# The reciprocal roots of a perceiver's batch loop: from ScalarE's Sqrt to Newton steps on VectorE

## The reference, cut to what matters

```
xn  = layernorm(context, ln_x_g, ln_x_b)          # rows of 512
ln  = layernorm(layernorm(x), ln_l_g, ln_l_b)
q   = ln @ Wq ;  k, v = (concat(xn, ln) @ Wkv)    # 822 keys
out = softmax(mask(q k^T / 8)) v                  # 16 heads
x   = x + tanh(g) * layernorm(out @ Wout, ln_o_g, ln_o_b)
layernorm(t) = (t - mean(t)) * rsqrt(var(t) + 1e-5)
```

## Time and profile before

| | us |
|---|---|
| median of 3 runs | 2095.2 (2090.87 to 2096.77) |
| the profiled execution | 2099.28, its span 2097.6 |
| PE busy | 1910.5 (91%) |
| DVE busy | 1021.2 (49%) |
| ACT busy | 845.9 (40%) |
| POOL busy | 640.9 (31%) |

### The profile page before, as it was taken

The page is one execution under the profiler, slowest core; times in us unless marked ns, Lnnn a source line. Parts: engine busy times, 40 slices in busy tenths (PEclk is TensorE's granted clock), DMA queues, the critical chain, the costliest instruction groups (busy, mean ns, idle before and its releaser), DMA issues. The chain is left out here.

```text
span 2097.6 us, 35149 instructions
## 1 busy us (share of the span) xinstructions
PE 1910.5 (91%) x12136; PEld 1551.3 (74%) x12136; DVE 1021.2 (49%) x2213; ACT 845.9 (40%) x1776; POOL 640.9 (31%) x519
## 2 busy tenths in 40 slices
PE   5689999999999999999859999999997885999994
PEld 3367878777777778787648888888884665999983
DVE  5324646464645555554464323333336556554564
ACT  3134434443434434434434323333322534565550
POOL 1203020202020020200034445555422203688872
PEclk9799999999999999999969999999998986999997
DMA  8642121211121212100053313333349125454646
GB/s 223 191 162 67 53 58 53 62 53 30 42 69 37 77 37 59 27 17 18 5 185 114 109 59 109 110 105 110 120 157 307 41 69 183 146 201 152 209 144 204
DMA packets 125590, 218.84 MB, mean 104 GB/s; under 512 B 40335, under 2 KB 41135, under 8 KB 124931
## 3 DMA queue, kind: packets, MB, share of 16 engines
q1 hardware_dynamic: 120643, 201.21, 29.8%
q0 software_dynamic: 4800, 15.73, 2.2%
HBM read 188.87 MB, written 28.04 MB: 103 GB/s over the span
## 5 line engine op out<-in xcount | busy, mean ns | idle before, releaser
L485 POOL TENSOR_TENSOR a_cols<-a_cols,a_moments_b 128x722 f32<-128x722 f32 x32 | 57.4, 1792 | 600.3 <-DMA a_moments_b<-a_moments_dram 600.3
L641 PE MATMUL a_kv_ps<-a_kvin_hi,a_wk_hi 128*128 128x512 f32 (+1 forms) x512 | 196.9, 385 | 12.3 <-DVE a_kvin_lo L889 12.3
L1094 PE MATMUL f_banks<-f_wab_hi,f_x_hi 128*128 x448 | 183.6, 410 | 2.8 <-DVE f_x_lo L1781 2.3
L643 PE MATMUL a_kv_ps<-a_kvin_hi,a_wk_lo 128*128 128x512 f32 (+1 forms) x512 | 180.6, 353 | 0.0
L642 PE MATMUL a_kv_ps<-a_kvin_lo,a_wk_hi 128*128 128x512 f32 (+1 forms) x512 | 180.4, 352 | 0.0
L1096 PE MATMUL f_banks<-f_wab_hi,f_x_lo 128*128 x448 | 176.4, 394 | 0.0
L1095 PE MATMUL f_banks<-f_wab_lo,f_x_hi 128*128 x448 | 175.9, 393 | 0.0
L563 ACT ACTIVATE a_probs<-a_probs,a_neg_max 100x822 f32<-100x822 f32 x128 | 125.9, 984 | 118.6 <-DVE a_neg_max L913 118.4
L1803 DVE TENSOR_TENSOR f_h_sb<-f_h_sb,f_banks 128x256 f32<-128x256 f32 x112 | 47.2, 421 | 239.9 <-ACT f_h_sb L1526 237.5
L1526 ACT ACTIVATE f_h_sb<-f_banks 128x256 f32<-128x256 f32 x112 | 43.1, 385 | 292.0 <-PE f_banks L1096 288.0
L641 PE MATMUL a_kv_ps<-a_wv_hi,a_kvin_hi 128*128 128x512 f32 (+1 forms) x384 | 157.2, 409 | 3.3 <-DVE a_k_lo L906 3.3
(11 more groups left out here) (409 smaller groups left out, 4825.2 us busy)
## 6 DMA issues: line engine op xcount, KB each, us to landing
f_raw<-f_pieces SPq DMA_DIRECT2D x94, 256.0 KB, 2.6
m_raw<-m_pieces SPq DMA_DIRECT2D x92, 256.0 KB, 2.8
f_wab_raw<-f_pieces SPq DMA_DIRECT2D x42, 512.0 KB, 6.2
m_wab_raw<-m_pieces SPq DMA_DIRECT2D x42, 512.0 KB, 6.1
a_cols<-ctx_cols SPq DMA_DIRECT2D x8, 1444.0 KB, 7.7
a_rows<-ctx SPq DMA_DIRECT2D x8, 1280.0 KB
a_moments_b<-a_moments_dram SPq DMA_DIRECT2D x8, 722.0 KB
ahead_piece<-g_ctx SPq DMA_DIRECT2D x2, 2880.0 KB, 20.4
```

The lines of the kernel that those rows point to most:

```text
L641: nc.tensor.matmul(out, hi_l, hi_r, start=first, stop=False)
L643: return nc.tensor.matmul(out, lo_l, hi_r, start=False, stop=last)
L1094: nc.tensor.matmul(out, left_hi, right_hi, start=start, stop=False)
```

## The change

In the loop, VectorE computes the reciprocal root by itself. `spread_rooted` adds epsilon, forms minus half of the variance, takes the first guess from the bits (a shift by one, then a constant minus the result, on integers), and makes 3 Newton steps y = y (1.5 - 0.5 v y y) of three instructions each: 13 instructions, 12 of them linked. ScalarE's `deviations` calls in the loop are gone. The roots before the loop and after it stay with ScalarE, with the number to wait for as an argument.

The place moves as well: before, VectorE's reciprocal stood at the head of the step after (pair 1, 3, 6); now the chain stands at the end of pair 0, 2, 5, behind the second division.

```
+            def spread_rooted(first, end):
+                m = slice(first, end)
+                var, y, h = mean_var[:, m, 1], root[:, m], less_half[:, m]
                 dev[0] += 1
-                dve.wait_ge(std_done, dev[0])
+                dve.wait_ge(var_done, dev[0])
+                own.link(nc.vector.tensor_scalar(var, var, EPS, None, ALU.add))
+                nc.vector.tensor_scalar(h, var, -0.5, None, ALU.mult)
+                own.link(nc.vector.tensor_scalar(y.bitcast(I32), var.bitcast(I32), 1, None, ALU.logical_shift_right))
+                own.link(nc.vector.tensor_scalar(y.bitcast(I32), y.bitcast(I32), -1.0, float(0x5F3759DF), ALU.mult, ALU.add))
+                for step in range(STEPS):
+                    own.link(nc.vector.tensor_tensor(var, y, y, ALU.mult))
+                    own.link(nc.vector.tensor_tensor(var, var, h, ALU.mult))
+                    own.link(nc.vector.scalar_tensor_tensor(var if step == STEPS - 1 else y, var, 1.5, y, ALU.add, ALU.mult))
...
-                    if hp == 0:
-                        if i + 1 < B:
-                            deviations(0, CT + 1)
-                        else:
-                            deviations(NEXT_IN, NEXT_IN + 1)
-                    if hp == 2 and i:
-                        deviations(OUT, OUT + 1)
-                    if hp == 5 and i == B - 1:
-                        deviations(NEXT_IN, NEXT_IN + 1)
...
-                    if hp == 1:
-                        if i + 1 < B:
-                            spread(0, CT + 1)
-                            dve.sem_inc(moments_done, 1)
-                        else:
-                            spread(NEXT_IN, NEXT_IN + 1)
-                        if i >= 2:
-                            normalise_next(i - 2)
+                    if hp == 1 and i >= 2:
+                        normalise_next(i - 2)
...
                     if hp == 3 and i:
-                        spread(OUT, OUT + 1)
                         finish(i - 1)
...
+                    if hp == 0:
+                        if i + 1 < B:
+                            spread_rooted(0, CT + 1)
+                            dve.sem_inc(moments_done, 1)
+                        else:
+                            spread_rooted(NEXT_IN, NEXT_IN + 1)
+                    if hp == 2 and i:
+                        spread_rooted(OUT, OUT + 1)
+                    if hp == 5 and i == B - 1:
+                        spread_rooted(NEXT_IN, NEXT_IN + 1)
```

More of the change, by code:

```diff
@@ L7 @@
 U8 = mybir.dt.uint8
+I32 = mybir.dt.int32
 ALU = mybir.AluOpType
@@ L154, in perceiver_attention @@
         std = sb("std", [P, CT + 2])
+        root = sb("root", [P, CT + 2])
+        less_half = sb("less_half", [P, CT + 2])
         l_stats = sb("l_stats", [P, B, 6])
@@ L241, in perceiver_attention @@
         halves = (slice(0, HD), slice(HD, P))
+        STEPS = 3
+        VARS = 2 * B + 3
         OWN = [2, 1, 2, 1, 1, 1, 0, 0]
@@ L505, in _, with deviations @@
             act.wait_ge(const_done, 5)
[L506 to L511, removed]
+            def deviations(n, first, end):
+                act.wait_ge(var_done, n)
                 nc.scalar.activation(std[:, first:end], mean_var[:, first:end, 1], ACT.Sqrt, bias=eps[:, :]).then_inc(std_done, 1)
@@ L585, in _ @@
                                      bias=bias_l[:, k:k + 1]).then_inc(lat_t_done, 1)
-            deviations(0, CT)
+            deviations(1, 0, CT)
             for u in range(PAIRS):
@@ L632, in _ @@
             move_t(PAIRS * B - 1, 1)
-            deviations(OUT, OUT + 1)
-            deviations(NEXT_IN, NEXT_IN + 1)
+            deviations(VARS - 1, OUT, OUT + 1)
+            deviations(VARS, NEXT_IN, NEXT_IN + 1)
             move_next(B - 1)
@@ L863, in _ @@
             dev = [0]
-            def wait_std():
+            def spread_rooted(first, end):
+                m = slice(first, end)
+                var, y, h = mean_var[:, m, 1], root[:, m], less_half[:, m]
                 dev[0] += 1
-                dve.wait_ge(std_done, dev[0])
+                dve.wait_ge(var_done, dev[0])
[7 more added lines that the diff above has]
+                    own.link(nc.vector.scalar_tensor_tensor(var if step == STEPS - 1 else y, var, 1.5, y, ALU.add, ALU.mult))
             def moments(p, tiles):
@@ L879, in moments, with spread @@
                 return ins
-            def spread(first, end):
-                wait_std()
+            def spread(n, first, end):
+                dev[0] += 1
+                dve.wait_ge(std_done, n)
                 own.link(nc.vector.reciprocal(mean_var[:, first:end, 1], std[:, first:end]))
@@ L1007, in _ @@
             moments(0, range(CT)).then_inc(var_done, 1)
-            spread(0, CT)
+            spread(1, 0, CT)
             dve.sem_inc(moments_done, 1)
@@ L1082, in _ @@
             project(B - 1).then_inc(var_done, 1)
-            spread(OUT, OUT + 1)
+            spread(2, OUT, OUT + 1)
             finish(B - 1)
@@ L1086, in _ @@
             moments_next(B)
-            spread(NEXT_IN, NEXT_IN + 1)
+            spread(3, NEXT_IN, NEXT_IN + 1)
             normalise_next(B - 1)
+            assert dev[0] == VARS
             keep_logits(B - 1)
```

## The result

The changed kernel takes 2081.3 us (median of 4 runs, 2081.14 to 2082.74) and the kernel before 2096.0 (4 runs, 2090.87 to 2100.61). The two medians differ by 14.7 us. The ratio on record is 0.9941, with a 95% interval of 0.992 to 0.9962: 12.4 us less, 8 to 17 by the interval. The forecast was 2085 on a median of 2095.2, that is 10.0 less.

A forecast was written before the change was run, and what follows sets the result against it. TensorE, busy 91% of the span, was taken as the bound, so only its waits counted: 6.4 + 1.0 + 2.6 = 10.0 us off the median of 2095.2 gives 2085; range for 8 in 10: 2079 to 2092.

The forecast's parts named there:

- (a): Pair 3, batches 1 to 7: without the Exp table load, seven score waits for the low keys go, 6.4 us.
- (b): Pair 1: batch 0's wait of the values' projection for the low keys goes, 1.0 us; nothing in batches 1 to 7.
- (c): Batch 7, pairs 5 and 6: value-tile wait of 1.32 goes, last score wait falls from 3.73 to 2.45; together 2.6 us.
- (d): The other table loads, behind pairs 0 and 2: worth nothing, since TensorE's work covers them.
- The chain: 13 small VectorE instructions behind pairs 0 and 2: 2.5 us, at most 3.9, hidden under cover, 0 on the path.
- this surplus: Pair 2: waits of 2.3 us where a division meets GpSimd's work on the context columns, to stay as before.
- rival 1: TensorE's clock follows idle times, in the last pair and pair 5: 2080, or 2090 if all five pairs fall; chance 0.14.
- Rival 2: Pair 3: GpSimd's delayed bias step meets VectorE's first division, 0.9 us lost in each of 7, 2091; chance 0.11.
- Rival 3: Pairs 3 and 1: VectorE's chain outlasts its cover of 4.5 and 5.6 us; 2109 at 0.6 an instruction; chance 0.05.
- Rival 4: TensorE never waited for the loads; another input, the copies out of PSUM, keeps the wait: 2095; chance 0.04.
- The sign that I had named against myself: Stages after 1060 us, whose instructions are the same: a length change over a few us would show the forecast wrong.

The follow-up runs named there:

- the moments first: The changed kernel, with SyncE storing and spreading the next batch's moments ahead of its wait for the previous batch's attention: 2080.3 us, ratio 0.9935 to the kernel before.
- the last run: The changed kernel with moments spread before SyncE's attention wait and routing bias added to logits before context columns are prepared: 2065.8 us, ratio 0.9873 to the kernel before.
- 12-step run: The changed kernel with 12 Newton steps instead of 3, 40 small instructions a chain instead of 13: 2111.2 us, ratio 1.0083 to the kernel before.

## Why the prediction was right, step by step

(a) Seven waits of the scores in pair 3, 6.4 us by the earlier trace rows: the pairs lost 0.97 or 0.98 each, 6.8. I take the 0.07 beyond the idle time of 0.90 for what the count of idle time leaves out at its edge; no run shows it apart. Batch 0 as the check of what a pair without a load costs (11.38) was exact.

(b) Pair 1 of batch 0, 1.0: measured 1.2. It keeps its 16.83 where only pair 3's loads go, and is back at 16.81 with all loads back. Pair 1 of the other batches: nothing, as said.

(c) Batch 7, pair 6: 2.6 against 2.9. The wait of 1.32 went, and the last wait fell from 3.73 to this:

```profile
1017.93 0.48 PE L707 MATMUL a_s_ps<-a_k_hi,a_q_hi 64*100 64x512 f32 x2 [2.33 <-DVE a_k_lo L912]
```

2.45 had been forecast. The load there costs 1.40, that is 0.12 more than its own 1.28; what the 0.12 are is open. The 1380 ns of drain that the Trainium skill gives beside a load ("ScalarE: Activation LUTs", "What ACT_TABLE_LOAD costs") would have made this 2.66; the trace disagrees here, where the load has nothing to wait for but the activation before it.

(d) The other loads: nothing. The run with the loads back shows it for pair 0's; for the Sqrt behind pair 2 it is read from ScalarE's idle time.

The chain: 2.38 us against 2.5, in pair 3 with 2.8 us of slack left behind it. The spacing of 0.20 on 8 elements held for 1 and 7 elements and, within 0.02, for the integer steps.

What I did not forecast. Pair 2 grew by 1.0 in the profiles. It moves by the start of GpSimd's work against the division: over the eight profiles with the old order of SyncE's queue pair 2 of batches 1 to 6 scatters between 14.17 and 15.5, and with the moments first it stands still. The forecast called this surplus unchanged. I take it for chance of the execution, of up to 1.3 us a pair: the changed kernel and the one with 48 copies more have the same loop, and their seven pairs take 103.9 and 102.0. Pair 0 of batch 0 was 1.2 shorter; its stretch from 113.5 to 124.5 has a granted clock of 0.53 before and of 0.69 after. It is 47.0 to 47.4 in the eight experiments as well, with the loads (47.22) and without. So the loads are not its cause, and the long one was the profile of before.

The last pair. After the shorter wait TensorE ran at half speed (1.2 GHz of 2.4) for 3.4 us, where before it did so from 1028.3 for 6.8, and the pair up to the end of its stage is 1.3 shorter. The stretch of half speed in the changed kernel:

```profile
1019.00:1022.40 3.40, 3.40 (x37) 2.90 (x34) 0.69 (x2) 0.00 (x0) 0.00 (x0) 0.52 0.00 0
```

That looks like rival 1 on this pair, but the shorter wait isn't the cause. In the run with only the output norm's root replaced the wait is the old one, and yet half speed lasts as briefly as here:

```profile
1017.95 0.47 PE L716 MATMUL a_s_ps<-a_k_hi,a_q_hi 64*100 64x512 f32 x2 [3.73 <-DVE a_k_lo L923]
```

```profile
1019.00:1022.40 3.40, 3.40 (x37) 2.96 (x34) 0.70 (x2) 0.00 (x0) 0.00 (x0) 0.54 0.00 0
```

The last pair takes 27.80 us there and 27.79 with all loads back, also behind 3.73 us of idle, against 27.78 in the changed kernel. In the last run it takes 26.23 behind the same 2.33 as in the changed kernel, and the clock doesn't fall at all:

```profile
1004.00:1007.40 3.40, 3.40 (x40) 2.27 (x37) 0.66 (x2) 0.50 (x1) 0.00 (x0) 1.00 0.00 0
```

So the length of half speed here is not set by the length of the wait, and the 1.3 us came by the luck of the two profiled executions. The clock of pair 5, the other part of the rival, did not move: two of five such pairs fell in both profiles (batches 4 and 5 before, 2 and 6 after). Over the profiles of the kernels that keep these waits it was 1 to 4 of the five, and none where the waits are gone.

The rivals. Rival 1: neither part is shown as an effect of the change. Rival 2: the mechanism exists and missed by 0.34 us in the nearest batch (by 0.6 in batch 4, where 0.3 had been forecast); 1.75 us more of chain bring it, for 0.5 to 0.6 us a pair where 0.9 had been put. The Trainium skill's rule for it ("SBUF — State Buffer", the reading notes on the port diagram) is that of VectorE and GpSimd the one that starts first has the shared pair of ports for its whole instruction and the other is blocked. The trace agrees, for both orders: a division of 0.65 turns to 1.73 beside a bias step of 1.30 that starts 0.01 ahead, and the bias step to 1.74 where the division is ahead by 0.07. Only the price is a little less than the rule would give: the blocked division ends 0.44 us after the bias step, not 0.65. Rival 3: the mechanism is true too, its price was too high. The 12-step run has 2111, where 2109 had been worked out for a chain of 7.2; for its chains of 7.6 behind pair 2 and 8.05 behind pair 0 the same working gives 2118. The cover was 2.4 + 2.8 = 5.2 us behind pair 2 of batch 4 and 2.6 + 3.6 = 6.2 behind pair 0, against 4.5 and 5.6. The prediction had read pair 3 in a profile in which a division of 1.82 us had made pair 2 late (0.4), had taken 0.75 for a normalisation that takes 0.55, and 0.3 off each for no stated reason. Rival 4 falls with the run that has the loads back.

The sign that I had named against myself, stages behind 1060 us changing by more than a few us, came near with 4.3; ten profiles of the same code scatter there by 11 us, so it was too narrow a sign for one pair of executions.

The result lies 3.7 below the forecast, 2.4 by the ratio. Of these 0.9 are in the three terms. The rest is within the interval of the ratio, 8 us wide, and nothing that the change did is known for it: the forecast's mechanism and its terms are shown, and that the whole came out so near is in part luck.

## What to carry to other kernels

A table load costs what the most critical reader behind the next activation loses, not its 1.28 us: of 32 removed, 22 had cost nothing and ten gave 10.9 us, and the number to add up is the idle time in front of the reader, or the load where that is shorter. A chain of small dependent instructions is cheap where its engine already waits for another; work out the slack to the first instruction that another engine waits for, and look which third engine's work the delay pushes onto what. Once a wait is understood, look whether the order in the same engine's program holds others: here one call moved ahead of another was worth as much again as the whole change. And a gain that one pair of profiles shows outside the places of the change is held against the other runs before it gets a cause: here the last pair had a good reason and the wrong one.

## What the runs showed of the hardware

- Small linked VectorE instructions (1 to 7 elements a partition, float or int32) take 0.14 to 0.17 us and start 0.18 to 0.21 apart, up to 39 links in a row.
- A Sqrt on one element a partition with its load costs ScalarE 1.28 + 0.20, and 1.28 again for the next Exp; the load takes 1283 ns at every one of the 32 places.
- A division of 0.65 us that starts 0.01 behind a GpSimd instruction of 1.30 takes 1.73, and 1.62 beside one of 1.76 that has 1.2 us left. All 66 divisions of over 0.8 us in the ten profiles end 0.44 or 0.45 us after a GpSimd instruction. A division that is 0.07 us ahead keeps its 0.65, and GpSimd's instruction takes 1.74; three that were ahead by 0.03 or less were late all the same.
- The granted clock falls behind some idle times of 2.06 us and not behind others in one and the same program; behind none where TensorE stays busy in those pairs. Behind idle times of 2.33 us it fell in one run and not in another, and the half speed behind 3.73 us lasted 6.8 us in one execution and 3.4 in another.
